# Local transformer block on Trainium2: inverse roots on VectorE by two quadratics, and the score mask as eight products of 64 rows by 32 columns

## What is computed

```python
def attn_layer(x, Wqkv, qs, ksc, Wo):
    q, k, v = jnp.split(x @ Wqkv, 3, -1)             # 16 heads of 64
    q = l2norm(q) * qs                               # t / max(norm(t), 1e-12)
    k = l2norm(k) * ksc
    q = q * cos * scale + rotate_half(q) * sin * scale
    k = k * cos * inv + rotate_half(k) * sin * inv
    out = local_attention(q, k, v)   # each window of 32 sees itself and the one before
    return out @ Wo

# local_attention
sim = jnp.einsum('bhwie,bhwje->bhwij', bq, bk2) * QK_SCALE
sim = jnp.where((it < jb) | (it > jb + w) | (jb == -1), -jnp.finfo(sim.dtype).max, sim)
attn = jax.nn.softmax(sim, -1)
```

## Time and profile before

| | us |
|---|---|
| median of 3 runs | 4272.27 (4267.4 to 4280.25) |
| the profiled execution's own time | 4279.95 |
| its span, first to last instruction | 4278.2 |
| TensorE busy | 3950.0 (92%) |
| VectorE busy | 3287.6 (77%) |
| GpSimd busy | 2977.4 (70%) |
| ScalarE busy | 2637.3 (62%) |
| mean granted TensorE clock | 0.971 |

### The profile page before, as it was taken

How to read it: one execution, slowest core, us unless ns; L and a number is a source line. 1 busy time by engine, 2 the same in 40 slices (tenths; PEclk the granted TensorE clock), 3 DMA queues, 4 the chain that set the end, 5 groups by cost and what they waited for, 6 DMA issues and landing times. The chain is left out here.

```text
span 4278.2 us, 151283 instructions
## 1 busy us (share of the span) xinstructions
PE 3950.0 (92%) x66376; PEld 2888.7 (68%) x66376; DVE 3287.6 (77%) x4155; ACT 2637.3 (62%) x3184; POOL 2977.4 (70%) x3649
## 2 busy tenths in 40 slices
PE   8999969999999999999878887799999999999997
PEld 5655657777777777777633333577777777777775
DVE  4535568888888888888668884688888888888885
ACT  4424436667767666666537774367667767667664
POOL 2202158889888888888634440788888988888884
PEclk9999989999999999999979998899999999999998
DMA  4304332333233323322100000332333333233221
GB/s 152 126 10 141 110 92 79 80 94 84 79 87 86 86 76 87 88 69 73 40 11 1 1 1 1 110 84 78 87 79 86 89 82 89 74 87 84 75 68 37
DMA packets 169727, 316.93 MB, mean 74 GB/s; under 512 B 39336, under 2 KB 43056, under 8 KB 166640
## 3 DMA queue, kind: packets, MB, share of 16 engines
q1 hardware_dynamic: 153520, 241.18, 20.8%
q0 software_dynamic: 15552, 66.07, 5.0%
HBM read 92.03 MB, written 20.05 MB: 26 GB/s over the span
## 5 line engine op out<-in xcount | busy, mean ns | idle before, releaser
L695 PE MATMUL psum<-loc_w_hl,loc_z_lo 128*128 128x512 f32 x1152 | 513.9, 446 | 39.5 <-DMA loc_w_hl<-parted 26.0
L1191 DVE TENSOR_REDUCE loc_ssq<-loc_sq 128x16 f32<-128x1024 f32 x384 | 464.6, 1210 | 24.2 <-POOL loc_rn L1074 24.2
L936 ACT ACTIVATE loc_sq<-psum 128x1024 f32<-128x1024 f32 x192 | 196.5, 1024 | 457.1 <-PE psum L697 452.0
L1078 POOL TENSOR_TENSOR loc_rc_k<-loc_rc_k,loc_rs_k 128x1024 f32<-128x1024 f32 x192 | 454.1, 2365 | 18.7 <-DVE loc_rs_k L1205 18.7
L1078 POOL TENSOR_TENSOR loc_rc_q<-loc_rc_q,loc_rs_q 128x1024 f32<-128x1024 f32 x192 | 459.1, 2391 | 0.0
L696 PE MATMUL psum<-loc_w_hl,loc_z_hi 128*128 128x512 f32 x1152 | 455.8, 396 | 2.1 <-issue 2.1
L1186 DVE TENSOR_TENSOR loc_rc_q<-psum,loc_rot 128x1024 f32<-128x1024 f32 x192 | 235.0, 1224 | 289.1 <-ACT loc_sq L931 159.9
L697 PE MATMUL psum<-loc_w_hl,loc_z_hi 128*128 128x512 f32 x1152 | 455.7, 396 | 0.2 <-issue 0.2
L792 PE MATMUL psum<-loc_PT,loc_V 64*64 64x32 f32 x24576 | 405.1, 220 | 7.3 <-issue 6.7
L792 PEld LDWEIGHTS psum<-loc_PT,loc_V 64*64 64x64 f32 x24576 | 381.2, 135 | 33.7 <-issue 10.1
L1097 POOL TENSOR_TENSOR loc_prob<-loc_prob,loc_recip 128x1024 f32<-128x1024 f32 x192 | 365.4, 1903 | 43.6 <-DVE loc_recip L1228 43.5
(11 more groups left out here) (198 smaller groups left out, 9616.7 us busy)
## 6 DMA issues: line engine op xcount, KB each, us to landing
loc_V<-loc_V SPq DMA_DIRECT2D x1152, 128.0 KB
loc_V<-loc_V SPq DMA_DIRECT2D x672, 64.0 KB
loc_w_hl<-parted POOLq DMA_DIRECT2D x72, 512.0 KB, 4.4
parted<-moe_halves POOLq DMA_DIRECT2D x18, 1024.0 KB, 5.2
moe_spread<-moe_gates SPq DMA_DIRECT2D x64, 256.0 KB, 4.0
moe_raw<-in_wqkv POOLq DMA_DIRECT2D x18, 512.0 KB, 6.3
moe_w<-in_moe_w SPq DMA_DIRECT2D x32, 256.0 KB, 3.3
loc_wo<-in_wo SPq DMA_DIRECT2D x12, 512.0 KB, 5.1
```

What stands on the lines that cost most here:

```text
L695: pe.matmul(M.bank[bank + g], z_lo[:, r, tokens], w[:, 0, cols], start=True, stop=False)
L1078: pool.tensor_tensor(rc, rc, rs[:, :], ALU.add).then_inc(added, 1)
L1191: dve.tensor_reduce(ssq[:, a:a + HEADS], heads(sq[:, :]), AX_X, ALU.add).then_inc(totalled, 1)
```

## The change

Three edits, all in the local block.

1. `root` moves from POOL to DVE, directly behind `guess`. With g the guess and t = g*g*ssq, the inverse root is now g times the product of two quadratics, (t*(t + a) + b) * (t*(t + c) + d), times a leading factor. That factor, `ROOT_LEAD`, is multiplied into the rotary tables on the host, so no instruction applies it. Six operations on 128x32 elements in place of ten; three semaphore waits on `root_step` and that on `guess_ready` stand between them. The guess now goes to a tile of its own (`rg`). POOL's `step` begins with the scaling of k.
2. The floor becomes a `scalar_tensor_tensor` with `ssq` as both inputs, where it was a `tensor_scalar`.
3. The mask products: eight instead of two. For each of the two banks (c) and each of the four windows (w), 64 rows of the identity by 32 of its columns give the 32 partitions of that window; the tile in the array is that of the score products of the same c and w. The opening window (tile 0, w = 0) takes the other half of the mask, and the host lays the two halves out accordingly.

```diff
@@ scores
                 for c in range(2):
-                    pe.matmul(M.bank[YB + c], M.ident16[:, :],
-                              M.mask[:, int(i > 0), :].rearrange("p (o k) -> p o k", o=1).broadcast_to([P, PAIRS, 2 * WINDOW]),
-                              start=True, stop=False, skip_group_check=True)
+                    r = 64 * c
+                    for w in range(TILES):
+                        seen = M.mask[r:r + 64, int(i + w > 0), :].rearrange("p (o k) -> p o k", o=1)
+                        pe.matmul(M.bank[YB + c][32 * w:32 * (w + 1), :], M.ident16[r:r + 64, r:r + 32],
+                                  seen.broadcast_to([64, PAIRS, 2 * WINDOW]), start=True, stop=False, skip_group_check=True)
@@ gpsimd
-            def root(L, t):
...
             def step(L, n, live):
-                if live(n - 1):
-                    root(L, n - 1)
@@ vector
             def floored(L, t):
...
-                dve.tensor_scalar(ssq[:, :], ssq[:, :], 1e-24, None, ALU.max).then_inc(floor_ready, 1)
+                dve.scalar_tensor_tensor(out=ssq[:, :], in0=ssq[:, :], scalar=1e-24, in1=ssq[:, :], op0=ALU.max,
+                                         op1=ALU.max).then_inc(floor_ready, 1)
...
-                dve.tensor_scalar(rn[:, :].bitcast(I32), ssq[:, :].bitcast(I32), -0.5, float(0x5F3759DF), ALU.mult,
+                dve.tensor_scalar(rg[:, :].bitcast(I32), ssq[:, :].bitcast(I32), -0.5, float(0x5F3759DF), ALU.mult,
                                   ALU.add).then_inc(guess_ready, 1)
+
+            def root(L, t):
+
+                step = (L * TS + t) * 5
+                (a, b), (c, d) = ROOT_FACTORS
+                dve.wait_ge(guess_ready, upto(L, t))
+                dve.tensor_tensor(rt[:, :], rg[:, :], rg[:, :], ALU.mult).then_inc(root_step, 1)
+                dve.wait_ge(root_step, step + 1)
+                dve.tensor_tensor(rt[:, :], rt[:, :], ssq[:, :], ALU.mult).then_inc(root_step, 1)
+                dve.wait_ge(root_step, step + 2)
+                dve.scalar_tensor_tensor(out=rv[:, :], in0=rt[:, :], scalar=c, in1=rt[:, :], op0=ALU.add,
+                                         op1=ALU.mult).then_inc(root_step, 1)
+                dve.scalar_tensor_tensor(out=ru[:, :], in0=rt[:, :], scalar=a, in1=rt[:, :], op0=ALU.add,
+                                         op1=ALU.mult).then_inc(root_step, 1)
+                dve.wait_ge(root_step, step + 3)
+                dve.scalar_tensor_tensor(out=rv[:, :], in0=rv[:, :], scalar=d, in1=rg[:, :], op0=ALU.add,
+                                         op1=ALU.mult).then_inc(root_step, 1)
+                dve.wait_ge(root_step, step + 5)
+                dve.scalar_tensor_tensor(out=rn[:, :], in0=ru[:, :], scalar=b, in1=rv[:, :], op0=ALU.add,
+                                         op1=ALU.mult).then_inc(root_ready, 1)
@@ vector, step
                     floored(L, n)
                     guess(L, n)
+                    root(L, n)
                 if live(n - 9) and lasts(n - 9):
                     add_ffn(L, n - 9)
@@ rotary_constants
-    tab = np.stack(tabs).astype(f)
+    tab = (np.stack(tabs) * ROOT_LEAD).astype(f)
@@ mask_constant
-    opening = (np.arange(P) < WINDOW)[:, None] & (k < WINDOW)
-    return np.concatenate([np.where(seen & ~opening, 0.0, MASKED), np.where(seen, 0.0, MASKED)], 1).astype(np.float32)
+    opening = seen & (k >= WINDOW)
+    return np.concatenate([np.where(opening, 0.0, MASKED), np.where(seen, 0.0, MASKED)], 1).astype(np.float32)
```

More of the change, by code:

```diff
@@ L59 @@
 NEWTON = 11
+ROOT_LEAD = 0.27406619329149995
+ROOT_FACTORS = ((-0.9034896806386632, 1.7067896912217941), (-4.2420135386446685, 5.265389317482745))
 def inverse_sqrt(dve, step, done, src, x, y, t, op, guard):
@@ L557, in local_transformer_block @@
         rc_k = sb("rc_k", [P, 2, INNER])
-        ssq, rn, rt, ru = (sb(n, [P, 2 * HEADS]) for n in ("ssq", "rn", "rt", "ru"))
+        ssq, rn, rg, rt, ru, rv = (sb(n, [P, 2 * HEADS]) for n in ("ssq", "rn", "rg", "rt", "ru", "rv"))
         qk_q, qk_k = (sb(n, [P, PAIRS, 2, DH]) for n in ("qk_q", "qk_k"))
```

## The result

The changed kernel takes 4312.33 us (median; 4303.2 to 4323.84), the kernel before 4275.96 on the same chip. The ratio is 1.0081, 95% interval [1.0058, 1.0105]: 0.8% slower, where 4197 us had been forecast. The profiled execution has a span of 4314.2 us, 36.0 more than before.

What follows compares the result with a forecast made beforehand. POOL was taken to set the pace at 15.89 us a step; afterwards DVE-POOL loop 15.39 plus friction 0.11 makes 15.5, gaining 0.39 x 192 = 75 us: 4197 us forecast, range 4125 to 4282.

Steps and rivals of the forecast that it cites:

- DVE's chain: Root on DVE: from the guess's start to the sine product's 1.24 us, where it was 0.09.
- POOL idle before the probabilities: Sign expected in each step: POOL waits some 2.8 us before the probabilities, ended by DVE's reciprocal.
- wait for the scaled q: Sign expected on PE: its weight loads no longer wait for POOL's scaled q, 22.3 us in 50 steps before.
- The waits for POOL: PE regains its waits for POOL: at least 0.35 us a step, at most 0.76.
- POOL's share: Sign expected: POOL's ten root operations gone and its busy share near 76% (11.8 of 15.5 us).
- The hold on DVE: DVE's guess cannot pass POOL operations on two tensors; its mean stays well over 0.18 us, ending on POOL's sum for k.
- that rival: POOL operations also hold DVE's root: about 8 us gained, about 4265 us; half of it some 4225; chance 0.16.
- The masks: Eight mask products on PE take 0.3 to 0.45 us against 0.36, gain taken 0.05 us a step.
- PE's pace after: PE's step: 15.89 less 0.35 to 0.76 of waits for POOL less 0.05 for masks, 15.1 to 15.5, middle 15.3 us.
- The DVE-POOL loop: Guess, root, reciprocal, probabilities, sum for k, next guess: 14.62 us, with extras 15.39 us a step, just over PE's 15.3.
- Nothing gained: other waits fill POOL's freed time: Rival: the time stays at 4272 us; chance 0.04.
- friction: Cost of two near-equal paces, DVE with POOL and PE, with unlike steps: 0.11 us, making the step 15.5 us.

Runs made afterwards that it cites:

- run 7: The changed kernel with the old two mask products and no root on any engine, raw guess used: 4345.72 us, 1.0148.
- run 9: The changed kernel with 128 semaphore increments on PE ahead of the local block's first work: 4345.85 us, 1.0157.
- run 8: The changed kernel with the old two mask products, plus ten idle POOL operations at the old root's place: 4302.25 us, 1.0044.
- runs 1: The changed kernel with the two old mask products, so only root and floor move: 4343.1 us, 1.013.
- Run 5: The kernel before with the copies of V held back until the next step's value products have ended: 4306.73 us, 1.0076.
- Run 2: The kernel before with the eight mask products alone, root still on POOL: 4297.53 us, 1.0014.
- runs 3: The changed kernel with POOL's weight loads issued behind the scaling of k: 4296.35 us, 1.005.
- run 6: The changed kernel with each copy of V cut to 64 of its 512 columns, output not the reference's: 4276.6 us, 0.9991.

## Why the prediction was wrong

**What held.** DVE's chain: sine product 1.23 us behind the guess (1227.42 to 1228.65), 1.24 forecast; each root operation 0.19. POOL idle before the probabilities 558.3/192 = 2.9 us, ended by the reciprocal, 2.8 forecast. No wait for the scaled q of any size. The waits for POOL, at 92.7/192 = 0.48 us a step, fell by 0.38, at the low end of the 0.35 to 0.76. POOL's share was 71%, for the 76% of a shorter step.

**The hold on DVE** was there, but the floor took it: 590 ns in the mean and 1.08 us at 1226.31, ending at 1227.39 where POOL's sum for k ends at 1227.33, while the guess fell from 408 to 253. I had left open whether the floor with two SBUF inputs is held. It is, and the Trainium skill's rule (SBUF — State Buffer, Who interferes with whom) agrees with it. The root's operations ran at 185 to 193 ns in the median, and of the 1152 only the first of the six was ever held, up to 671 ns (its mean is 202): that rival is out, and run 7 closes it.

**The masks** take 0.41 us (0.59 before), inside the 0.3 to 0.45 expected, but I had undersized the gain. From the first transposition of the probabilities to the first score product it was 1.45 us and is 1.20 (1225.56 to 1226.76): 0.25, not 0.05. I had moved a drain of 0.42 in front of the masks on the strength of the weight loads' idle time. PE's own row shows none, now or before: the masks start 0.06 us before the transposes end, and in the kernel before the first score product started at 1225.38, 0.07 us before the masks ended (1224.86 + 0.59). The weight loads stood idle while PE was busy with the masks; now they are idle 0.17 us in front of them. That may be the drain of the rule that I had cited, but it is no time of PE that moves. The span model of the Trainium skill (TensorE: Matmul & The Clock Gate, Measured speedup vs the span model), by which I had named 0.4 and a gain of 0.15, was the nearer.

**The step that failed** is "PE's pace after": 15.89 less the waits for POOL less the masks. It takes every microsecond that PE stops waiting for POOL as a microsecond gained. It isn't: in those waits PE's instructions arrived, and the wait for them took their place. In the stretch from 800 to 1585 us the stops at every 256th instruction make 1.2 us of each 16.4 us step (0.2 of each 15.8 in the kernel before); what is left, 15.2, is the pace that the prediction gave to PE alone (15.1 to 15.3). The DVE-POOL loop, whose 15.39 the sum was built on, doesn't show as the pace: run 7 takes the root's 1.2 us out of it and gains nothing. The prediction read the views of POOL, DVE and PE's releasers and passed over the row "L766 <- issue 25.8", and with it nearly all of what grew. Among the rivals it stood as "Nothing gained: other waits fill POOL's freed time", with a chance of 0.04 and no change as its price; none of the rivals had it as a loss. The "friction" of 0.11 us a step was the place for it in the sum; the waits on "issue" grew by 121.3/192 = 0.63, and the projections' rows by 25/192 = 0.13.

**Why the whole lost less than that stretch says.** 0.5 us in each of 192 steps would be 98 us; the span grew by 36. The stretch from 800 us on is worse than the mean: over both local blocks, by the starts of POOL's scaling of k, a step grew from 15.85 to 16.13 us, 53 us in 190 periods. In groups of 12 steps the changed kernel needs 180 to 201 us where the kernel before needs 186 to 193; the two groups with the least time in stops behind the first of each block (9.7 and 11.7 us) are as fast as before (191.3 for 191.8, 190.8 for 190.5). The other 17 us lie outside these steps, 14 of them ahead of the first (573.4 us for 587.4). The change doesn't touch that part. In ten traces (all but run 9, which puts its increments there) the first product of the local block starts anywhere from 560 to 574 us, early and late with the old root's place as with the new, so these 14 us can't be put down to the change, and what it costs in the steps may be nearer 53 us than 36. Each figure is from one execution.

**Why removing waits made it slower, and not just equal.** The span's +36.0 is, by the table, 121.3 of waits on "issue" and 6.8 of other waits, less 72.7 of waits for POOL and 20.8 of busy time (34.6). Of that busy time the masks alone would have given 37.0 (115.9 to 78.9), but the half clock took part of it back. That stops cost more than the waits they replace is measured (run 8 against runs 1 and 7). Half clock follows stops of PE of whatever cause, 211 times of 211; so it doesn't go by the sum of the instruction stops alone. Run 5 has 85.3 us of it with only 58.9 us of these stops: 10 of its 19 stretches stand behind waits for transfers, mostly of the FFN's weights, and 6 behind waits for POOL. Run 2 has 81.9 us with 95.3, half of its 23 stretches behind POOL; runs 3, 6 and 9 have 51 to 61 us with 175 to 199. How much of the 36 us is half clock and how much idle time was not told apart.

**What stays open.** What decides when a packet starts. Theory D says that dense runs outrun the packets; it doesn't say why 36% of the packets start over 2 us late in the changed kernel and 23% in the kernel before, and most of the lost time lies behind these. Run 8 shows that holding PE back brings the share down, run 6 that the copies of V don't set it (34% with a third of the traffic). No run here told more. Nor did any beat the kernel before by more than the measurement can tell; the best that keep the root on DVE and compute the reference are runs 8 and 3 (1.0044 and 1.005).

## What to carry to other kernels

Before you count a removed wait as gained, ask what else was arriving in it. Where an engine runs hundreds of tiny instructions back to back, look for idle time that ends on "issue" in the middle of one loop. If it lies at a fixed count of instructions, supply is the bound, and what makes that engine freer can make it grow, as here. What to try then is fewer instructions, or slow work between the dense runs, before a shorter dependence chain; neither was tried here. Idle instructions put in front cost their time and only moved the stops. And count a stop of TensorE at more than its own length where half clock follows it.

## What the runs showed of the hardware

- PE's instructions came in packets of 16,384 bytes, 256 instructions each; a packet took about 1.1 us (median), and PE could go on 2.6 us after its start. Every stop of more than 0.34 us inside a score or value run, in both kernels and all nine runs, lay at remainder 193 of 256.
- 256 instructions of 64-row products take 1.5 to 2.1 us, less than the 2.6 us of one packet; in the changed kernel a stop there was 1.25 us in the mean and 3.2 at most, from start to start. Of all stops in the local blocks (208 us), 134 us lay where the packet had started more than 2 us after PE's entry into the block before.
- Half clock came 22 times in the changed kernel's local blocks, 21 of them for 3.4 us, and 34 times in the one with no root; before it was 9. Each of the 211 times in eleven traces it began in a stop of PE of over 1 us or less than 3 us behind one, whether PE had waited for instructions, POOL, DVE or a transfer.
- An instruction that only increments a semaphore is recorded at 51 ns but 128 in a row started 151 ns apart.
- A DVE operation with two SBUF inputs of 32 elements a row took 0.19 us in the median and up to 2.06 us beside POOL operations on two tensors: the 82 of the 192 new floors that lasted over 0.3 us all ended within 0.12 us of the end of a POOL operation.
